# Front and attention of a transformer block as one program: the fold's last group computed head by head among the first steps of attention, and the score banks swapped

## What is computed

```python
mod = (silu(c) @ wmod)                       # sa, ca, ga, sb, cb, gb: shifts, scales, gates
h = layernorm(x) * (1 + ca) + sa             # x: 2 x 1024 tokens x 512 channels
q = rmsnorm(rope(h @ Wq_c @ Wq_up))          # 16 heads of 128
k_sw, v_sw = rmsnorm(rope(h @ Wk)), h @ Wv   # one key and one value head
ck = rmsnorm(blocks_of_16(h) @ W_comp)       # 64 compressed keys a batch
c_out  = softmax([q @ ck.T * scale, sink]) @ ck            # masked by block
sw_out = softmax([50 * tanh(q @ k_sw.T * scale / 50), sink]) @ v_sw   # window of 128
inter = einsum('btgf,gfi->btgi', c_out + sw_out, Wg)       # 4 groups of 4 heads
x = x + ga * (inter @ Wo)
x = x + gb * ffn(layernorm(x) * (1 + cb) + sb)
```

## Time and profile before

| | |
|---|---|
| three runs | 1029.49, 1029.59, 1030.93 us; median 1029.59 us |
| the profiled execution | 1023.58 us, of which span 1021.5 us |
| mean granted clock of TensorE | 0.962 of 2.4 GHz |
| front, with the fold | 0 to 172.2 us of the span |
| attention | 172.2 to 738.3 us |
| feed-forward | 738.3 to 1021.5 us |

### The profile page before, as it was taken

How to read it: one execution, slowest core, us unless ns; L and a number is a source line. 1 busy time by engine, 2 the same in 40 slices (tenths; PEclk the granted TensorE clock), 3 DMA queues, 4 the chain that set the end, 5 groups by cost and what they waited for, 6 DMA issues and landing times. The chain is left out here.

```text
span 1021.5 us, 16023 instructions
## 1 busy us (share of the span) xinstructions
PE 930.4 (91%) x4766; PEld 777.5 (76%) x4766; DVE 677.1 (66%) x1256; ACT 564.8 (55%) x1556; POOL 560.1 (55%) x760
## 2 busy tenths in 40 slices
PE   4989886699999999999999999999668999999996
PEld 4987774577888888887788888888457777878784
DVE  4565495488888888888888888888568442332312
ACT  0554452477777777777777777777231423324221
POOL 0175000588888888888888888887213222222222
PEclk9799898699999999999999999999879999999999
DMA  8757652304024131131221402420180020020101
GB/s 272 225 205 240 255 171 90 114 16 142 17 57 138 46 112 47 57 126 37 88 91 42 142 17 57 139 65 11 43 349 0 1 83 1 1 83 1 42 0 43
DMA packets 52738, 93.66 MB, mean 92 GB/s; under 512 B 9920, under 2 KB 29376, under 8 KB 49728
## 3 DMA queue, kind: packets, MB, share of 16 engines
q1 hardware_dynamic: 42192, 65.30, 20.0%
q10 hardware_dynamic: 10480, 27.47, 7.4%
HBM read 75.33 MB, written 26.08 MB: 99 GB/s over the span
## 5 line engine op out<-in xcount | busy, mean ns | idle before, releaser
L968 PE MATMUL banks<-fold,aoT 128*128 128x512 f32 x768 | 194.2, 402 | 1.4 <-DVE aoT L1149 1.4
L1506 PE MATMUL banks<-hT,w_hi 128*128 128x512 f32 x704 | 172.3, 397 | 14.9 <-DVE w_hi L1555 13.0
L1506 PEld LDWEIGHTS banks<-hT,w_hi 128*128 128x128 f32 x704 | 132.6, 191 | 44.6 <-issue 13.1
L1647 POOL TENSOR_TENSOR gus<-arena,gus 128x512 fp32r<-128x512 f32 x44 | 59.5, 1353 | 194.0 <-ACT gus L1549 194.0
L968 PEld LDWEIGHTS banks<-fold,aoT 128*128 128x128 f32 x768 | 140.7, 190 | 29.5 <-DVE aoT L1149 1.8
L968 PE MATMUL banks<-k_st,qT 128*128 128x320 f32 (+6 forms) x768 | 123.7, 311 | 0.0
L1615 DVE SCALAR_TENSOR_TENSOR arena<-banks,sg,arena 128x512 f32<-128x512 f32 x44 | 33.0, 749 | 122.6 <-ACT arena L1544 122.6
L968 PEld LDWEIGHTS banks<-k_st,qT 128*128 128x128 f32 x768 | 110.0, 192 | 0.2
L1544 ACT ACTIVATE arena<-banks,sg 128x512 f32<-128x512 f32 x44 | 30.3, 689 | 136.4 <-PE banks L1506 136.4
L1473 PE MATMUL banks<-w_hi,gus 128*128 128x512 f32 x352 | 90.8, 398 | 10.8 <-POOL gus L1647 8.7
L968 PE MATMUL banks<-pp,v_st 128*128 128x512 f32 x360 | 99.5, 410 | 0.0
(11 more groups left out here) (185 smaller groups left out, 1971.2 us busy)
## 6 DMA issues: line engine op xcount, KB each, us to landing
arena<-in_wq_blocks ACTq DMA_DIRECT2D x8, 1056.0 KB, 4.9
wq_words<-in_wq_blocks ACTq DMA_DIRECT2D x8, 1056.0 KB, 7.0
w_lo<-wq_words SPq DMA_DIRECT2D x11, 768.0 KB, 14.2
go_raw<-in_w_go SPq DMA_DIRECT2D x16, 512.0 KB, 5.7
arena<-in_L_attn_h SPq DMA_DIRECT2D x16, 256.0 KB, 5.6
comp_raw<-in_w_comp SPq DMA_DIRECT2D x16, 256.0 KB, 5.3
v_parts<-v_out ACTq DMA_DIRECT2D x4, 1024.0 KB, 4.5
k_st<-k_parts SPq DMA_DIRECT2D x32, 128.0 KB, 2.5
```

The costliest lines, as they stand in the source:

```text
L968: last = pe.matmul(out, lhs[a], rhs[b], start=start and q == 0 and u == 0, stop=stop and q == n - 1 and u == 2)
L1506: last = pe.matmul(GU[2 * (n % 2) + w][:], parts[a][:, h, cols], hT[:, c % 2, x, k], start=(k == 0 and q == 0), stop=(k == KC - 1 and q == ...
L1647: pool.tensor_tensor(gus[:, n % 2, 1], gu[:, n % 2], gus[:, n % 2, 0].bitcast(F32), ALU.subtract).then_inc(gu_lo, 1)
```

## The change

The front and attention become one block: `front_programs` and `attention_programs` give five functions each, and every engine runs the front's and then attention's without a barrier between them. Four things come with that.

- **The fold's last group.** Steps 12 to 15 are still loaded and split, but `fold_step` runs only for steps 0 to 11. The last group is computed by head: a unit f is the 12 matmuls of head f over all four steps, in one bank (`UNIT_BANK`), and PE runs unit 0 ahead of q0, unit 1 behind q0, unit 2 behind q1 and unit 3 behind q3. ACT (`unit_high`) and DVE (`unit_low`) take each out in between. A unit needs the splits of all four steps (`go_lo` 13 to 16).
- **The banks.** Q, T, O, Y move to banks 4 to 7 and S to banks 0 to 3. The feed-forward block's `Y` and `GU` are swapped alike.
- **SP's order.** The first two tiles are loaded behind `load_go(11)`, ahead of the loads 12 to 15 of the fold; x, `sg` and the rest follow.
- **The rest.** `row` is multiplied behind step 11 instead of step 14. DVE waits for the last split before it writes attention's constants. ACT issues the first load of feed-forward weights before its first step. Attention's buffers that take the place of the fold's are ones not used in its first steps.

```diff
-            with ExitStack() as scope:
-                front_block(nc, scope, ...)
-            with ExitStack() as scope:
-                attend_block(nc, scope, ...)
+            with ExitStack() as scope:
+                buffers = attention_buffers(sb, scope)
+                sem = semaphores(nc, scope)
...
+                @block.tensor
+                def _(pe):
+                    front.tensor(pe)
+                    attention.tensor(pe)
...
+UNIT_BANK = (0, 1, 6, 7)
+UNIT_FREE = (5, 6, 11, 12)
...
-        for n in range(10, STEPS):
-            load_go(n)
-        sp.wait_ge(zero_stored, 16 * (BATCH + 2))
+        for n in range(10, STEPS - HG):
+            load_go(sp, n)
...
-        fold_high(3)
...
-            elif n == 14:
-                dve.wait_ge(sd_in, 16)
+            elif n == 11:
+                dve.wait_ge(late_in, 32)
...
-        fold_low(3)
...
-        for n in range(3, STEPS):
+        for n in range(3, STEPS - HG):
             fold_step(n)
+
+    def unit(pe, f):
+
+        g = GPT - 1
+        pe.wait_ge(f_lo, UNIT_FREE[f])
+        for i in range(HG):
+            pe.wait_ge(go_lo, HG * g + i + 1)
+            for u, (a, b) in enumerate(((0, 0), (0, 1), (1, 0))):
+                last = pe.matmul(bank[UNIT_BANK[f]][:], go[:, i, a, f * P:(f + 1) * P], go[:, i, b, C:2 * C],
+                                 start=(i == 0 and u == 0), stop=(i == HG - 1 and u == 2))
+        last.then_inc(unit_mm, 1)
+
+    def unit_high(act, f):
+        act.wait_ge(unit_mm, f + 1)
+        act.activation(fold[:, H - HG + f, 0], bank[UNIT_BANK[f]][:], ACT.Copy).then_inc(f_hi, 1)
+
+    def unit_low(dve, f):
+        dve.wait_ge(f_hi, H - HG + f + 1)
+        dve.tensor_tensor(fold[:, H - HG + f, 1], bank[UNIT_BANK[f]][:], fold[:, H - HG + f, 0].bitcast(F32), ALU.subtract
+                          ).then_inc(f_lo, 1)
...
-    Q, T, O, Y = bank[0:4]
-    S = banks[:, 4:8]
+    Q, T, O, Y = bank[4:8]
+    S = banks[:, 0:4]
...
         def query(g):
+            if opening(g, 0):
+                units.unit(pe, 0)
+                pe.wait_ge(units.up_lo, 1)
+                pe.wait_ge(units.f_lo, 2 * HG + 1)
             wait(pe, f"q_in{g.tile_slot}", g.loaded())
...
+            for c, f in ((0, 1), (1, 2), (3, 3)):
+                if opening(g, c):
+                    units.unit(pe, f)
...
         def probs_high(g):
+            if opening(g, 0):
+                units.high(act, 3)
...
         def squares(g):
+            if opening(g, 0):
+                units.high(act, 0)
...
+            if opening(g, 0):
+                units.high(act, 1)
...
+        dve.wait_ge(units.rope_in, 32)
+        dve.wait_ge(units.sink_steps, 2)
+        dve.wait_ge(units.go_lo, STEPS)
         dve.memset(exponent[:], -0.5).then_inc(s["consts"], 1)
...
+        units.stored(sp)
+        for t in range(2):
+            load(t, t)
+        units.load_rest(sp)
+        sp.wait_ge(units.sd_done, 1)
+        for t in range(2):
+            load_x(t, t)
...
-    Y, GU = bank[0:4], bank[4:8]
+    GU, Y = bank[0:4], bank[4:8]
```

More of the change, by code:

```diff
@@ L21 @@
+from collections import namedtuple
 from contextlib import ExitStack
@@ L133, in build_program @@
             wup = sb(attn, "wup", [P, 2, H * D], F32R)
+            with ExitStack() as folding:
+                go_raw = sb(folding, "go_raw", [P, 4, 2 * C])
+                go = sb(folding, "go", [P, 4, 2, 2 * C], F32R)
+                raw_up = sb(folding, "raw_up", [P, H * D])
             with ExitStack() as scope:
[L135 to L137 removed]
@@ new lines, in build_program, with _ @@
+                attention = attention_programs(
+                    sem, buffers, units, banks, bank, x_tok, x_mid, q_parts, k_parts, v_parts, ck_parts, ckq_parts, table,
+                    kons, ident, low, wup, fold, sinkb, sink_e, ga, wq_blocks, wq_words, words_out, s_blocks, sg, arena,
+                    inexact, xs_ffn, xs_in, norm)
+                block = scope.enter_context(nc.Block())
+                @block.sync
+                def _(sp):
+                    front.sync(sp)
+                    attention.sync(sp)
@@ new lines, in attention_programs @@
+def attention_programs(sem, buffers, units, banks, bank, x_tok, x_mid, q_parts, k_parts, v_parts, ck_parts, ckq_parts, table, kons,
+                       ident, low, wup, fold, sinkb, sink_e, ga, wq_blocks, wq_words, words_out, s_blocks, sg, arena, inexact,
+                       xs_ffn, xs_in, norm):
+    MASKED, WHOLE = 0, 1
+    (logits, cs, prob, ws, wr, cmx, csm, crs, squares_w, flag, ones, minus_zero, pp, pcS, aoT, y_t, x_t, pc, q_st, rope_st, k_st,
+     v_st, ck_st, sq, ss, rq, exponent, epsilon, qn, ropb, qT) = (buffers[n] for n in (
+         "logits cs prob ws wr cmx csm crs squares_w flag ones minus_zero pp pcS aoT y_t x_t pc q_st rope_st k_st v_st ck_st sq "
+         "ss rq exponent epsilon qn ropb2 qT").split())
@@ L955, in steps, with opening @@
                 after[r]()
+    def opening(g, c):
+        return g.starts_batch and g.m == 0 and g.c == c
     def wait(engine, name, count):
@@ L1051, in project_first @@
             wait(pe, "ao_lo", g.n())
+            if opening(g, 0):
+                pe.wait_ge(units.f_lo, H)
             if g.j == 0:
@@ L1171, in probs_low @@
         def probs_low(g):
+            if opening(g, 0):
+                units.low(dve, 3)
             wait(dve, "p_hi", g.n())
@@ L1192, in query_low @@
             dve.tensor_tensor(qT[:, g.slot, 1], T[:], qT[:, g.slot, 0].bitcast(F32), ALU.subtract).then_inc(s["qT_lo"], 1)
+            if opening(g, 0):
+                units.low(dve, 2)
         def scale_query(g):
+            if opening(g, 0):
+                units.low(dve, 0)
             wait(dve, "q_rs", g.n())
@@ L1198, in scale_query @@
                               rq[:, g.slot].unsqueeze(2).broadcast_to([P, HG, D]), ALU.mult).then_inc(s["q_sc"], 1)
+            if opening(g, 0):
+                units.low(dve, 1)
         def compressed_sum(g):
```

221 lines of the change are left out of this document (109 added, 112 removed).

## The result

| | before | after |
|---|---|---|
| times, us | 1025.08, 1029.49, 1029.59, 1030.93 | 1011.99, 1012.66, 1013.82, 1017.44 |
| median | 1029.54 | 1013.24 |
| profiled execution, span | 1023.58, 1021.5 | 1013.82, 1012.0 |

The ratio is 0.9856, 95% interval 0.9815 to 0.9898. Between the two profiled executions it is 9.8 us. So the first question is where the other 6 us come from. Among the executions behind the numbers of this document three ran at a far lower clock (1544.88 us in e1, 1178.17 in e8, 1182.73 among the 23 of the kernel before beside e1): medians here include them, ratios and spreads leave them out.

The account below looks back on a forecast made before the run. PE, busy for 91% of the span, was taken as the bound, with time to be had at the passage from fold to attention. Terms summed to -10.0 us, from 1029.59 to 1019.6, range 1015.0 to 1025.0.

Parts of the forecast that it names:

- behind q4: Rest of attention, barrier and feed-forward after the fifth query: same work in the same order, taken to move along, 0.
- T: End of the fold's split 15 on DVE, 161.15 before: forecast 161.55, 0.4 later, bounds 0 and 2.9 later.
- q0 to q1: From first to second query on PE, 5.18 before: ACT perhaps 1 us later than the constants, +0.6.
- clock around unit 0: PE's clock may drop between pieces of unit 0, slowing the first query and unit 1: +0.7, bounds 0 and 1.5.
- q3 to q4: Fourth to fifth query: unit 3 on the path, partly at low clock, +3.2 to the second scores' end, then 0.
- q0 (T included): Start of the first query on PE: T + 0.75 = 162.3 instead of 174.66, -12.4.
- q1 to q2: From second to third query, 5.04 before: query matmuls at full clock bring ACT's squares forward, -0.4.
- q2 to q3: From third to fourth query, 9.18 before: query and first scores shorter at full clock, -1.7, at worst 0.
- the fold's loads come late: Rival, fold loads queued behind 14 small transfers: T at 164 to 167, at 165 a gain of 6.5, 1023.1; chance 0.2.
- The clock did not stay up: Rival, attention's opening: the clock stays up as PE has more to do, -13.1, 1016.5; chance 0.15.
- Attention's steps did not get dearer: Rival, the 60 steps after the fifth query: moved banks and buffers cost 0.3 us a step, 1037.6; chance 0.04.
- The gain reached the end: Its opposite was a rival: T 10 us late or a load holds the fifth query at its old place, 1029.6; chance 0.03.

Follow-up runs that it names:

- e1: The kernel before, unchanged, run again: 1027.44 us in twelve executions, ratio 0.9996.
- e8: Against the changed kernel: one program, the fold's last group computed in the front without units, banks not swapped; 1024.09 us, ratio 0.9970 to the kernel before.
- e2: The changed kernel, unchanged, run again: 1013.13 us in six executions, ratio 0.9861 to the kernel before.
- e10: The changed kernel, unchanged, profiled a fourth time: 1015.33 us.
- e5: The changed kernel with fold loads 12 to 14 issued ahead of the first two tiles' loads, load 15 behind them: 1016.12 us, ratio 0.9919 to the kernel before.
- e4: The changed kernel with unit 3 ahead of q3 instead of behind it: 1007.82 us in six executions, ratio 0.9817 to the kernel before.
- e12: The changed kernel with unit 3 ahead of q3, profiled a second time: one execution of 1020.54 us.
- e6: The changed kernel with unit 3 ahead of q3 and fold loads 12 to 14 ahead of the tiles' loads: 1011.17 us, ratio 0.9870 to the kernel before.
- e7: The kernel before, still two blocks, with only the banks swapped: 1027.38 us in twelve executions, ratio 1.0012.
- e3: Against the changed kernel: one program, swapped banks and new SP order kept, but the fold's last group computed in the front, no units; 1021.87 us, ratio 0.9946 to the kernel before.

## Why the prediction was wrong in its number

**The steps that failed.** 1013.2 lies 6.4 us below the 1019.6. Three parts of this can be named, the last without a cause.

- *The base, 1.8 us.* The last step of the prediction is: "The runs lie about 6 us above the profiled execution, at 1029.59; the same difference makes 1019.6." Nothing in a row stood for these 6 us. 2.7 of them are the early F of the profiled execution (143.66 against a mean of 146.4) and do belong into a median. But the three runs lay 1.8 above the median of the 23 later ones, and the forecast carried that along.
- *The worth of the change, 2.2 us.* What comes behind q4 was "taken to move with it", a term of 0. It measured -1.6, of which 1.2 lie in the steps q8 to q63. The sum up to q4 measured -10.6 instead of -10.0.
- *Open, 2.4 us.* 1019.6 less 1.8 and 2.2 makes 1015.6. The rest to 1013.2 is within the scatter of four executions (the 95% interval of the ratio, 0.9825 to 0.9897 in e2, is 7 us wide), and how much of it is chance stays open.

The range, 10 us wide, held bounds of the sum only and none for the spread of single executions, which the profile of one could not show. That the forecast for the profiled execution itself (1013.6, span 1011.5) met 1013.82 and 1012.0 is luck: that execution's F came 1.1 us later than in the profile of before, and in the sum to q4 a T that came 2 us later than forecast is made up by three terms that came out smaller (q0 to q1, the clock around unit 0, q3 to q4).

**The sum, term by term**, against the means behind F in the table (three profiles before, four after):

| term | forecast | measured |
|---|---|---|
| T | +0.4 | +2.4 |
| q0 (T included) | -12.4 | -10.3 |
| q0 to q1 | +0.6 | -0.8 |
| q1 to q2 | -0.4 | -0.5 |
| q2 to q3 | -1.7 | -1.6 |
| q3 to q4 | +3.2 and 0 | +2.6 |
| clock around unit 0 | +0.7 | 0 |
| sum to q4 | -10.0 | -10.6 |
| behind q4 | 0 | -1.6 |
| all | -10.0 | -12.2 |

- *T.* The rival "the fold's loads come late" was half right: +2.4, where its span began at 164 and T came at 164.49. SP sent load 12 at 151.97, 143.00 + 8.9 for fourteen issues, as I had it (151). What failed was the landing: I took 156 to 159 for the four, and the last was used at 162.18, some 8 us behind its issue. That is the 8.2 of the earlier trace rows, which I had as the bound and should have taken as the value: it was the only row for four queued loads. In e10 T was 3.6 later than before, above the bound of 2.9. By the Trainium skill, "DMA: Bandwidth & Descriptors", section "Queues, rings and completion order", each DMA engine consumes the descriptors of a ring in order, but a later one may finish its write before an earlier one. So the prediction's "load 12 moves no byte before the tiles' loads have" says more than that page does, and no row here shows the bytes of single loads. e5 agrees with the order, in that what was put last in the queue was what T waited for, but load 15 was also issued later there.
- *From T to q0* 0.85 to 0.87 in all four profiles, 0.75 forecast.
- *q0 to q1.* I let ACT come 1 us behind the constants because of the third group's output. ACT began that at 163.15, ahead of T, and was free at 165.2. q1 went as by DVE alone, 0.4 sooner even (T + 5.20, where T + 5.55 was the sum by DVE). The unit filled the wait, as forecast.
- *q2 to q3, q3 to q4.* The mechanism was right to the row. In the profiled execution q3 to the end of the second scores is 8.4 (182.02 to 190.40) against 5.36, +3.0 where 3.2 was forecast, and the rest to q4 is 5.4 as before. The other three profiles of after have 8.1, 8.3 and 7.5 (e10). e4 and e12 show the other side: with unit 3 inside the wait and 1.6 us of it left ahead of q3, q3 and the second scores ran at full speed, and q4 came 4.8 us sooner behind q3. The rule on the clock cited in the prediction (the Trainium skill, "TensorE: Matmul & The Clock Gate", section "HAM oscillation — how this bites in real kernels") agrees with this in kind: behind the wait of 4.32 us the burst ran cold, behind one of 1.6 it did not. But these rows give no border: in e10 the burst began at full speed, in e12 the half speed came behind the wait of 1.81 for `gus`, and q4 took 1.62 in all four profiles of after and 0.93 in e12, with about 2.3 us of idle time on PE shortly before it in each.
- *The clock around unit 0.* Pieces of 0.93 to 0.97 for three matmuls with waits of 0.3 to 1.3 between them: full speed. No drop, 0 instead of +0.7. In e5 and e6, where the wait there was 3.31 and 3.80, q0 did run slowly (1.49 and 1.48).
- *Behind q4, 0 forecast.* q8 to q63 is 454.3 to 454.9 in all ten profiles of kernels with one program, 455.5 to 455.95 in the four with two: 1.2 us. The swap is not the cause (e7: 455.74), nor are the units (e3: 454.43). What of the one program it is, I did not find. q63 to ffn is 1.6 shorter in the mean, but scatters from 49.9 to 52.6 among kernels with the same code there, so no cause is claimed. From ffn to the end after is 0.5 longer. Between q4 and q8 it lost 0.7, nearly all of it in the first profile: q4 ran at half speed in all four (1.62), but only there the scores behind it did too (3.43, where the others have 2.0).

**The rivals.** The clock did not stay up before q3 (the wait of 4.32 was there, as the forecast had it) but did so around unit 0. The loads came late and T with them, but the gain lost by it was made up elsewhere. Attention's steps did not get dearer. The gain reached the end.

## What to carry to other kernels

Before a forecast is turned from a profiled execution into a median, look for what places the profiled one: a mark ahead of the change splits the common scatter from the effect, and twelve executions settle what three cannot. A wait of 4 us in front of dense matmuls was paid twice here, once as idle time and once as half speed behind it, so loose work belongs ahead of the waiting instruction and not behind it. Joining two programs pays only in part by the border that goes (7 of 12 us behind F in one profile, 5.5 of 14 in the times); the rest comes from spreading the last work of the first over the waits of the second.

## What the hardware showed unexpectedly

The front runs the same instructions in every kernel, yet F scatters over 9.8 us. About 3 of these arise in one place. The second group of 32 small matmuls in PE's timeline, of the kernel before:

```profile
24.09 3.98 PE L725 MATMUL banks<-csil,comp_raw 128*128 128x2 f32 x32
```

And of e12:

```profile
24.63 6.83 PE L761 MATMUL banks<-csil,comp_raw 128*128 128x2 f32 x32
```

It takes 3.7 to 4.1 us or 6.83; the four profiles with 6.83 (e2, e7, e8, e12) have the four latest F: 151.25, 150.66, 147.22 and 151.84. The first group, ahead of it, takes 6.96 in all fourteen. So it looks as if the engine's speed rises at one of two moments; that is a reading of these durations and not shown. The granted clock of 20 to 32 us does not tell it: it reads 0.84 in before and 1.00 in e12, where the matmuls were slower. I have not found what decides between the moments, nor where the other 7 of the 9.8 us arise.

Feed-forward's opening has a second such place. POOL's first `gus` takes 2.91 us in e10 and e12 and 1.28 or 1.29 in the other twelve profiles, and only in these two does PE wait for it, 1.76 and 1.81. Beside it DVE's operation on `w_lo` takes 1.75 in both, and 2.86 in e4 and 2.87 in the first two profiles of after. So one of the two operations is stretched while the other runs at its usual length, and which one it is differs from execution to execution of the same code. Why is not shown.
